# A two-layer transformer block on one core: every remaining hardware loop of five stages written out turn by turn

## The reference

```
x = x + ga * L0_attn(h)     # 16 heads of 16, causal softmax, values gated by a small network
x = x + gb * L0_ffn(h)      # shared SwiGLU, and 8 experts of which the router keeps the best 2
x = x + ga * L1_attn(h)     # short convolutions, rotary, chunked delta rule (4 heads of 64, chunks of 32)
x = x + gb * L1_ffn(h)      # per-row quantised linear layer, 256 to 256
```

## Time and profile before

| | |
|---|---|
| median of three runs | 2902.31 us |
| the profiled execution | 2902.24 us |
| its span | 2900.4 us |
| TensorE busy | 2617.9 us, 90% |
| VectorE busy | 2259.8 us, 78% |
| ScalarE busy | 1627.7 us, 56% |
| GpSimd busy | 199.6 us, 7% |
| instructions in the record | 88193 |

### The profile page before, as it was taken

How to read it: one execution, slowest core, us unless ns; L and a number is a source line. 1 busy time by engine, 2 the same in 40 slices (tenths; PEclk the granted TensorE clock), 3 DMA queues, 4 the chain that set the end, 5 groups by cost and what they waited for, 6 DMA issues and landing times. The chain is left out here.

```text
span 2900.4 us, 88193 instructions
## 1 busy us (share of the span) xinstructions
PE 2617.9 (90%) x36424; PEld 1573.6 (54%) x36424; DVE 2259.8 (78%) x4398; ACT 1627.7 (56%) x2406; POOL 199.6 (7%) x228
## 2 busy tenths in 40 slices
PE   6889999999999999999999998999988998128996
PEld 3332566665666655665566524555545666116774
DVE  3559899999999998999999824565556999775887
ACT  2330677777777777777777791111116777216673
POOL 1238000000000000000000000000000000100000
PEclk8995899999999999999999998999998999659998
DMA  4234011011110111101110001000000333313441
GB/s 145 86 100 83 3 28 29 5 27 27 28 29 5 27 28 28 28 6 27 28 29 7 4 20 52 14 29 15 14 8 13 97 102 103 119 37 106 124 120 58
DMA packets 158639, 133.19 MB, mean 46 GB/s; under 512 B 103097, under 2 KB 135995, under 8 KB 153275
## 3 DMA queue, kind: packets, MB, share of 16 engines
q1 hardware_dynamic: 152571, 124.08, 17.8%
q10 hardware_dynamic: 4224, 4.19, 0.4%
q0 software_dynamic: 1536, 0.40, 0.1%
HBM read 79.98 MB, written 46.66 MB: 44 GB/s over the span
## 5 line engine op out<-in xcount | busy, mean ns | idle before, releaser
L709 DVE TENSOR_REDUCE attn_pm<-attn_MS 128x1 f32<-128x512 f32 (+3 forms) x2304 | 1331.7, 639 | 112.3 <-PE attn_MS L753 94.8
L695 ACT ACTIVATE attn_PT<-attn_ES 128x1024 f32<-128x1024 f32 (+5 forms) x1152 | 1040.7, 951 | 389.0 <-PE attn_ES L788 385.1
L803 PE MATMUL attn_OP<-attn_PT,attn_VH 128*17 128x512 f32 (+2 forms) x4608 | 638.8, 557 | 0.4 <-issue 0.3
L753 PE MATMUL attn_MS<-head_KX,head_QX 96*32 96x512 bf16 (+12 forms) x3456 | 397.2, 393 | 4.4 <-DVE attn_pm L709 3.5
L753 PE MATMUL attn_MS<-attn_KX,attn_QX 96*32 96x512 bf16 (+7 forms) x2880 | 317.0, 364 | 2.4 <-issue 1.1
L753 PE MATMUL attn_MS<-after_attention,attn_QX 96*32 96x512 bf16 (+7 forms) x2880 | 309.2, 358 | 1.5 <-DVE attn_pm L709 1.0
L788 PE MATMUL attn_ES<-head_QX,head_KX 99*32 99x512 bf16 (+6 forms) x3456 | 283.2, 360 | 7.8 <-ACT attn_PT L695 4.4
L788 PE MATMUL attn_ES<-attn_QX,after_attention 99*32 99x512 bf16 (+10 forms) x2880 | 241.8, 357 | 1.7 <-DMA attn_QX<-attn_parts 1.3
L788 PE MATMUL attn_ES<-attn_QX,attn_KX 99*32 99x512 bf16 (+8 forms) x2880 | 237.7, 357 | 0.0
L1189 PE MATMUL l0out_ring<-l0out_w,l0out_sT 128*128 128x512 f32 x512 | 224.9, 592 | 0.0
L753 PEld LDWEIGHTS attn_MS<-head_KX,head_QX 96*32 96x32 bf16 x3456 | 140.7, 97 | 135.6 <-DVE attn_pm L709 62.8
(11 more groups left out here) (295 smaller groups left out, 3341.2 us busy)
## 6 DMA issues: line engine op xcount, KB each, us to landing
vk_beta<-front_vk SPq DMA_DIRECT2D x8, 1024.0 KB, 4.0
kq_transposed<-l0out_w_in SPq DMA_DIRECT2D x8, 1024.0 KB, 4.8
delta_VK<-vk_beta SPq DMA_DIRECT2D x32, 256.0 KB, 2.8
delta_QK<-kq_transposed SPq DMA_DIRECT2D x32, 256.0 KB, 2.9
attn_QX<-qk_parts SPq DMA_DIRECT2D x60, 128.0 KB, 7.7
after_attention<-attn_out SPq DMA_DIRECT2D x18, 256.0 KB
x_res<-in_L_attn_x_dram ACTq DMA_DIRECT2D x8, 512.0 KB, 8.0
qk_parts<-project_hi SPq DMA_DIRECT2D x8, 512.0 KB, 2.9
```

Source lines behind the costliest of these rows:

```text
L695: nc.scalar.activation(PT[u % NPT][:, 512 - wa:512 + wb], ES[half][:, 512 - wa:512 + wb], ACT.Exp, scale=DH ** -0.5).then_inc(exp_done, 1)
L709: nc.vector.tensor_reduce(pm[r][:, i, c:c + 1], MS[slot][:, 0:w], AX.X, ALU.max).then_inc(max_taken, 1)
L753: last = nc.tensor.matmul(MS[slot][r, 0:seen], QX[b][0:ROWS, i * P + 32 * g:i * P + 32 * g + 32], KX[b][0:ROWS, 512 * c:512 * c + seen], s ...
L803: last = nc.tensor.matmul(OP[32 * j:32 * j + DH + 1, 512 - w:512], VH[b][:, kt, :], PT[(2 * n + half) % NPT][:, o:o + w], start=(kt == 0), ...
```

## The change

Every `with engine.Fori(a, b) as i:` that was left becomes `for i in range(a, b):`, in all five engines' streams. The loop's body is then produced once for each turn, with the turn as a Python number. No work, order, buffer, semaphore or size changes. For the 12 looped turns of the recurrence on TensorE this is 12 copies of the body in the place of one.

```
--- before.py
+++ after.py
@@ -227,7 +227,7 @@
-            with sp.Fori(0, G) as g:
+            for g in range(0, G):
@@ -281,7 +281,7 @@
-            with act.Fori(0, G - 1) as g:
+            for g in range(0, G - 1):
@@ -290,7 +290,7 @@
-            with pool.Fori(0, G) as g:
+            for g in range(0, G):
@@ -351,7 +351,7 @@
-            with dve.Fori(0, G - 1) as g:
+            for g in range(0, G - 1):
@@ -394,7 +394,7 @@
-            with pe.Fori(0, G - 1) as g:
+            for g in range(0, G - 1):
@@ -619,7 +619,7 @@
-            with sp.Fori(0, TURNS) as i:
+            for i in range(0, TURNS):
@@ -968,9 +968,9 @@
-            with sp.Fori(1, G - FIRST) as g:
+            for g in range(1, G - FIRST):
-            with sp.Fori(G - FIRST, G) as g:
+            for g in range(G - FIRST, G):
@@ -1114,10 +1114,10 @@
-            with dve.Fori(0, G - FIRST - 1) as g:
+            for g in range(0, G - FIRST - 1):
-            with dve.Fori(G - FIRST, G - 1) as g:
+            for g in range(G - FIRST, G - 1):
@@ -1497,7 +1497,7 @@
-            with act.Fori(1, G // 2 - 1) as i:
+            for i in range(1, G // 2 - 1):
@@ -1689,7 +1689,7 @@
-            with dve.Fori(3, G - 1) as n:
+            for n in range(3, G - 1):
@@ -1833,7 +1833,7 @@
-            with pe.Fori(1, G // 2 - 1) as i:
+            for i in range(1, G // 2 - 1):
@@ -1987,7 +1987,7 @@
-            with sp.Fori(3, NU - 1) as i:
+            for i in range(3, NU - 1):
@@ -2017,7 +2017,7 @@
-            with pool.Fori(1, NU) as n:
+            for n in range(1, NU):
@@ -2112,7 +2112,7 @@
-            with act.Fori(2, NU - 1) as i:
+            for i in range(2, NU - 1):
@@ -2333,7 +2333,7 @@
-            with dve.Fori(3, NU - 1) as i:
+            for i in range(3, NU - 1):
@@ -2540,7 +2540,7 @@
-            with pe.Fori(3, NU - 1) as i:
+            for i in range(3, NU - 1):
```

## The result

The changed kernel takes 2925.82 us (median of 4 runs, 2922.24 to 2929.24), the kernel before 2901.95 us in the runs beside it: 1.0075 times, with a 95% interval from 1.0062 to 1.0087, which is 18 to 25 us. The prediction was 2903.5 us with a range to 2917, so the time lies outside it, on the side of the second rival and 7 us beyond that rival's worst case. The profiled execution is the slowest of the four, 2929.24 us.

The account below looks back on a forecast made before the run. TensorE fills attention and the expert stage, VectorE is fullest in the front, and a chain of waits bounds the recurrence. 2902.24 − 3.9 − 0.7 − 1.3 + 7.2 = 2903.5 us, range 2893 to 2917.

Parts of the forecast that it names:

- the second rival: Recurrence: late code pages stall TensorE in full, 0.39 us a packet, 11.3 to 22.6 us; 2907.6 to 2918.9 us; chance 0.30.
- What does one cost?: Recurrence, price of fetching TensorE's written-out code: 28.8 new packets at 0.25 us each, 7.2 us more.
- One crossing in three: Recurrence: three of nine code packets show a TensorE stall, 1.18 us on average, so 9.6 stalls are expected.
- The slack takes 0.69 us of two thirds of them: Recurrence: two of three stalls stand before L2449, whose 0.69 us wait for VectorE absorbs part, leaving 0.49 us.
- turn 2 has no such piece: Recurrence: turn 2, read as written out, shows no TensorE piece waiting for nothing; taken as support for hidden fetches.
- the first rival: Code fetches are hidden in the recurrence as in attention: 2896.3 us, or 2892.2 with uncovered branches; chance 0.22.
- Registers and branch in the recurrence, 1.3 us less: Recurrence: VectorE's L2162 follows L2361 0.11 us sooner in 12 turns; TensorE's branch is hidden; bounds 0 and 3.9 us.
- Projection, 3.9 us less: Projection: three steps behind a finished partner shorten by 0.09, 0.35 and 0.12 us, 0.56 in 7 looped turns; bounds 0 to 7.0.
- VectorE's front, 0.7 us less: Front: register steps at VectorE's L1573 and L1605 save 0.17 us in each of 4 looped turns; bounds 0 and 1.4 us.
- Expert stage and attention at nothing: Neither stage changes: TensorE's queued work covers the expert branch and fetches, between −1.5 and +1.3 us; attention's SyncE transfers run ahead.
- The other engines' fetches at nothing: Recurrence: some 10 packets of the other engines' code in 12 turns cost nothing, at most 3.9 us.
- over 17.1 us: Recurrence sign: turns this long, where about 16.9 us was forecast, would mean code fetches stall in full.

## Why the prediction was wrong, step by step

- *The step that failed is "What does one cost?" in the term for fetching the code*: 0.25 us a packet, 7.2 us. The count was right: 28.8 new packets were expected in the recurrence and 29 came (42 for 13). The size of a stall was right too: 1.18 us from the earlier trace rows, 16.6 / 14 = 1.19 us in the changed kernel. Three things were wrong. *One crossing in three* was a count over nine packets of a stretch in which the turns aren't yet full, and three of the nine (at 2656.55, 2663.18 and 2670.65 us) come after TensorE has entered the loop (the MOVE of L2543 is at 2655.8 us); six with three stalls are left. In eleven full turns 14 pieces stand against 29 packets, every second one. *The slack takes 0.69 us of two thirds of them*, and leaves 0.49, was argued, not read. It would have been 4.4 us of 11.3, and was 2.1 of 16.6. That VectorE, for which L2449 waits, is held up by the same stall, as the second rival said, fits this and was not isolated. *A stall costs only its own length* was never put as a step: TensorE's busy time rose by 7.50 us in eleven turns, of which the lower clock is 3.9 us (1.5 of 4.52 in the kernel with TensorE alone written out) and the rest some 0.2 us at each piece. The price as the runs have it is 19.2 / 29 = 0.66 us a packet, and 23.9 us over 29, 0.82, in the changed kernel, with intervals that overlap.
- *Two readings behind this term were off.* The earlier trace rows calls its stretches turns 1, 2 and 3; they are turns 2, 3 and 4. L2468 runs from turn 3 on alone, and the trace has it at 2659.43 us. So the second stretch, called written out, is the loop's first pass, and "turn 2 has no such piece", the first rival's support, was read from looped code; so was a part of the 1.15 us a turn of the second. And the upper end of the range takes 0.72 us for each of 28.8 packets, where 0.72 was the mean of a stall, of which 9.6 were expected.
- *The second rival* had the mechanism and its sign, at 0.39 to 0.78 us a packet and 0.30; it lacked the clock and the added busy time, and its upper end, 2918.9 us, was 7 us low. Its other support, traffic that slows a fetch, is not shown: a packet takes a median of 0.98 to 1.15 us in the recurrence and 1.08 to 1.15 in quiet attention.
- *The first rival* (fetches hidden as in attention) fell. 209 packets in attention cost next to nothing, 29 in the recurrence cost 19 to 24 us. What differs can be read from where the pieces stand: L2439, L2404, L2414, L2427 and L2457, none at L2361, L2391 or L2378. L2414 and L2439 are 32 products each in 0.58 and 0.39 us. I counted TensorE's recorded instructions from the program's start, in the order in which they began. In the kernel with TensorE alone written out all 13 pieces of the eleven turns come at place 233 or 234 of each 256, and in the changed kernel all 14 at place 193 or 194. They end 2.2 to 2.9 us after a packet has begun, one of them 3.2. Where the engine reached that place 3.2 us or more after the packet's start there is no piece, and at six crossings of 2.3 to 2.8 us none either. So a page that is asked for while the engine runs through dozens of tiny products comes too late, and one that is asked for among large ones does not. That the request goes out a fixed number of instructions ahead was not tried.
- *Registers and branch in the recurrence, 1.3 us less*: right, 16.40 to 16.29 us a turn once TensorE's code is not fetched.
- *Projection, 3.9 us less*: the three steps were right (20.31 to 19.77 a turn, 0.54 for 0.56), and the sum was wrong, since the clock fell in three or four of the shortened turns. *VectorE's front, 0.7 us less*: the wait of L1573 is gone from the trace, but the front took 337.8 us for 335.7, and no run isolates it. *Expert stage and attention at nothing*: right for the turns; the expert turns did not move by 0.01 us, and attention took 1.4 us more, in one trace of each kernel, which no run isolates. *The other engines' fetches at nothing*: right.
- Of the signs named beforehand, the turns "over 17.1 us" and the issue pieces came as the second rival had them: 200.96 / 11 = 18.27 us.

## What to carry to other kernels

Before a loop is written out, ask what its body's instructions are: work that hides register steps hides them in either form, but a body that repeats from the engine's own memory costs no fetch, and a written-out one of many tiny products does. Count the pages (256 records on TensorE) and look in stretches that are already written out, and long ones, for pieces of "issue". And price every new stall of TensorE, and every gain that only shifts its idle time, together with the clock that follows it.

## What the runs showed of the hardware that I had not expected

- The body of a hardware loop is kept up to a size between some 1,400 and 2,090 instructions on TensorE; above it all of its pages are fetched in each pass (24 and 23 packets in 140 us, none below), and turns with the branch back take 2 to 5 us more than their neighbours.
- A fetch that comes late costs 1.2 us on average and up to 2.7 us in the changed kernel, and 0.2 us of added busy time. The clock was 0.50 behind its three longest pieces; in the kernel with TensorE alone written out it was 0.50 behind one of 1.53 us and stayed at 1.00 behind the longest, 2.11 us.
- The clock at the start of a turn can differ between turns with the same 2.04 us of idle time before them; with 1.88 us of useless products in that gap it was 1.00 in every turn from the second, and the kernel was 10.9 us faster together with the written-out loops (0.9955 times, 0.9941 to 0.9969), of which the trace places 5.6 us in the projection.
